# A new order for one unit of an attention kernel: value products two steps at a time, other TensorE work placed between raw score pairs

## The chip, the cores and the metric

The kernel runs on one core of a Trainium2 chip. The metric is the device time of one execution in microseconds, the median of several runs. The engines are TensorE (PE, with its weight loads as PEld), VectorE (DVE), ScalarE (ACT), GpSimd (POOL) and SyncE (SP), which here only issues transfers.

## What is computed

A cross-attention over 8 batches of 256 channels by 512 positions with 16 heads of 16 channels, followed by a mixture of experts (8 experts, two chosen for each of 2048 rows). Cut to what matters here:

```python
q = Wq @ target + bq; k = Wk @ source + bk; v = Wv @ source + bv     # target is layernorm(x)
dot = einsum('bhdt,bhds->bhts', q, k) / sqrt(16)
dot = mask * dot - (1 - mask) * 1e6
out = einsum('bhts,bhds->bhdt', softmax(dot) * mask, v)
x = x + out
x = x + experts(layernorm(x))          # softmax gate, top 2 of 8, silu(g) * u, down projection
```

## The kernel before

**Units.** The attention is cut into 16 units, one for each 128 rows (8 heads) of each batch. Units 0 and 1 have orders of their own (the start); units 2 to 15 run `unit(u)`, once on each engine, and unit 15 is the `TAIL`. Behind the last unit come the experts, whose code the change does not touch but for one product.

**What TensorE does in a unit.** A unit has eight steps s of four heads or blocks j. `scores(u, s, j)` makes one 128x512 tile of transposed scores in one of three banks `sc`; ScalarE takes its exponential into the buffer `pr` of the step; `product(u, s)` multiplies the four tiles of a step with the values, four 32-column products side by side, accumulated in the bank `pvb`. Four steps make one half of the unit's output, which ScalarE copies to `ov`. In the same unit TensorE makes the *raw* scores of a later unit, `raw_scores(u, w, m)`, 16 pairs of 128x512 for each unit, of which VectorE takes the maxima (`maximum`, one reduction for each pair). The maxima go through a transposition (`transpose_maxima`), a split into three bf16 parts on VectorE (`split_maxima`) and a transfer (`keep_maxima` on SP) into rows of `qk`, and `scores(u + 1, 0, 0)` waits for them.

**The pairs.** Unit u makes the pairs m = 4 to 15 of unit u + 1 and then m = 0 to 3 of unit u + 2. I count them i = 0 to 15 within a unit, so that i = 12 is the first pair of unit u + 2. It waits for that unit's rows of `qk`: `pe.wait_ge(stacked[m // 8].sem, ...)` for m = 0, which is the landing of `stack(u + 2, 0)`; i = 4 waits in the same way for `stack(u + 1, 1)`.

**Other TensorE work of a unit.** `values` (16 small f32 products), `project(u, 0)` and `project(u, 1)` (query and key projections of unit u + 3), `transpose_tokens`, `logits` and `ranks` (the expert choice of unit u - 2). They and the raw pairs share two PSUM buffers `tile` in turn: a tile may be written when VectorE (for `transpose_tokens`, ScalarE) has read the tile before the last one.

**What sets the order.** All orders are written out by hand, one for each engine, and an engine's queue runs in order. SP's order in a unit is

```python
store_product(u - 1, 1); keep_split(u, 1); load_product(u); store_x1(u)
store_recip(u)          # waits for rec_made "m", which reciprocals(u, 1) on VectorE raises
stack(u + 2, 0)         # two transfers, of 768 KB and of 8 KB
store_product(u, 0); load_recip(u); keep_split(u, 0); keep_maxima(u + 1, ALL)
```

(left out: its waits, and what comes first, `stack(u + 1, 1)` and loads). `reciprocals(u, 0)` and `reciprocals(u, 1)` are two small VectorE instructions on the softmax denominators of unit u - 1. In the profile `maximum` is L990, the second reciprocal instruction L974, `store_recip` L507, `stack` L453 and L456, `keep_maxima` L526, `scores` L1507, `raw_scores` L1519, `product` L1545.

Of the kernel before, what the change touches and what calls it, by code (L numbers as in the profile page):

```python
# [8 lines left out]
BF16 = mybir.dt.bfloat16  # L9
# [8 lines left out]
P = 128  # L18
# [30 lines left out]
VALUES_AT = 1, 0  # L49
NSLOT = 2  # L50
# [49 lines left out]
def pairs_of(n, s):  # L100

    if 0 <= n < len(FRONT):
        at = 3 * s if s < 4 else 2 * s + 4
        return FRONT[n][at:at + (3 if s < 4 else 2)]
    first = LEAD + 2 * s
    w, m = (n + 1, first) if first < NPAIR else (n + 2, first - NPAIR)
    return [(w, m), (w, m + 1)] if has(w) else []


def maxima_of(n, s):  # L110

    front = {(0, 1): (0, 1), (0, 4): (1, 0), (1, 1): (1, 1)}
    if (n, s) in front:
        return [front[n, s]]
    return [(n + 1, ALL)] if n > 0 and s == 6 and has(n + 1) else []
# [6 lines left out]
def fillers(n, s):  # L122

    return ((["v"] if s == VALUES_AT[n > 0] and has(n + 1) else []) + (["q"] if s == 3 and has(n + 3) else [])
            + (["xT"] if s == 3 and has(n - 2) else []) + (["logits"] if s == 4 and has(n - 2) else []))


def tile_events(n):
    ev = []
    for s in range(8):  # L130
        max_ = [(n, ("max", *pair)) for pair in pairs_of(n, s)]
        ev += max_[:1]
        if s == 7 and has(n - 2):
            ev.append((n, "ranks"))
        ev += max_[1:]
        ev += [(n, name) for name in fillers(n, s)]
# [5 lines left out]
        if s == 7 and has(n + 3):  # L142
            ev.append((n, "k"))
        if n == TAIL and s == 2:
            ev.append((n, "early"))
        if n == LAST - 1 and s == 7:
            ev.append((n, "count"))
# [70 lines left out]
def attention(nc, load_expert, x, ctxt, mask, maskc, maskd, wq, wk, wv, bq, bk, bv, gate, ident, ut, iotas,  # L218
# [3 lines left out]
    with st:  # L222
# [14 lines left out]
        mall = sb("mall", [B, T])  # L237
        mrow = sb("mrow", [B, 2, T], BF16)
# [13 lines left out]
        pr = [sb(f"pr{i}", [P, 4, T]) for i in range(2)]  # L252
        ov = sb("ov", [P, 2, T])
        mx = sb("mx", [P, 2, 32])
# [82 lines left out]
        def of(ahead, *names):  # L337
# [12 lines left out]
                for h in range(2)]  # L350
# [33 lines left out]
                 (mall[:, :], mask, mask_in))  # L384
# [265 lines left out]
        def _(pool):  # L650
# [160 lines left out]
        def _(act):  # L811
# [94 lines left out]
        def _(dve):  # L906
# [250 lines left out]
            def unit(u):  # L1157
                maximum(u, u + 1, 4)
                normalize(u - 1)
                maximum(u, u + 1, 5)  # L1160
                values_out(u)

                maximum(u, u + 1, 6)
                token_stats(u, 0)
                maximum(u, u + 1, 7)
                token_stats(u, 1)

                maximum(u, u + 1, 8)
                token_normalize(u, 0)
                maximum(u, u + 1, 9)  # L1170
# [670 lines left out]
```

## Time and profile before

| what | value |
|---|---|
| median of 3 runs | 869.19 us (865.51 to 871.01) |
| the profiled execution, as timed | 871.53 us |
| its span on the core | 869.7 us |
| TensorE busy | 801.8 us, 92% |
| VectorE busy | 553.6 us, 64% |
| ScalarE busy | 318.6 us, 37% |
| GpSimd busy | 370.3 us, 43% |
| mean granted clock of TensorE | 0.972 |

The profile is one execution; its busy times are shares of the span. What the time is worth in a unit is read from the stretches of that unit, since the start, the attention units and the experts have different limits. The units 2 to 13 take from 121.85 to 504.85 us, the experts from about 557 us to the end.

### The profile page before, as it was taken

How to read it: one execution, taken by the hardware profiler on the slowest of the kernel's cores; microseconds unless marked ns; L12 is line 12 of the kernel's file. 1: busy time of each engine (PE TensorE's matmuls, PEld its weight loads, DVE VectorE, ACT ScalarE, POOL GpSimd, SP SyncE). 2: the span in 40 equal slices, each digit the busy share in tenths (PEclk: the TensorE clock that was granted, in tenths of full speed). 3: DMA queues.
4: the chain of work that ended last, by engine and by line, in shares of the span. 5: the costliest groups of instructions: out<-in, count | busy, mean ns of one | idle time of the engine just before them, and what ended most of it. 6: DMA issues, size and time to landing. Idle time of an engine off the chain costs nothing. (4 is left out here: it accounts for less than half of the span.)

```text
span 869.7 us, 13002 instructions
## 1 busy us (share of the span) xinstructions
PE 801.8 (92%) x3757; PEld 365.1 (42%) x3758; DVE 553.6 (64%) x1071; ACT 318.6 (37%) x619; POOL 370.3 (43%) x392
## 2 busy tenths in 40 slices
PE   5888898989999998999989988899999999999993
PEld 2322332333333433433333332365555665665661
DVE  5778887889888887888877874445433333333331
ACT  0035465556565565665655666522000000000000
POOL 7544364556565655655745423334211221211221
PEclk9579999999999999999999999999999999999997
DMA  6745577666766866856845542354648546354332
GB/s 188 231 129 145 172 203 221 200 209 210 231 206 184 264 196 182 257 163 177 244 127 160 172 113 83 94 144 110 152 89 227 133 110 172 65 156 72 72 51 34
DMA packets 84524, 138.02 MB, mean 159 GB/s; under 512 B 14765, under 2 KB 40685, under 8 KB 84474
## 3 DMA queue, kind: packets, MB, share of 16 engines
q1 hardware_dynamic: 68970, 108.65, 41.8%
q0 software_dynamic: 7744, 17.86, 10.7%
q10 hardware_dynamic: 7760, 10.89, 4.5%
q8 instruction: 25, 0.41, 0.2%
q14 instruction: 25, 0.20, 0.1%
HBM read 77.36 MB, written 59.36 MB: 157 GB/s over the span
## 5 line engine op out<-in xcount | busy, mean ns | idle before, releaser
L843 ACT ACTIVATE pr<-sc 128x512 f32<-128x512 f32 x512 | 267.1, 603 | 219.5 <-PE sc L1507 219.3
L990 DVE TENSOR_REDUCE mx<-tile 128x2 f32<-128x1024 f32 x256 | 309.0, 1216 | 55.9 <-PE tile L1519 50.3
L1507 PE MATMUL sc<-qk 100*128 100x512 bf16 x512 | 154.8, 384 | 9.9 <-DMA qk<-mxt 7.2
L1519 PE MATMUL tile<-qk 97*128 97x512 bf16 x496 | 150.9, 388 | 14.0 <-DVE mx L990 7.9
L765 POOL DMA_INDIRECT out_dram<-xin,ids x36 | 56.4, 1566 | 224.0 <-DVE ids L1312 220.0
L1545 PE MATMUL pvb<-pr,vp 128*32 128x512 f32 x1024 | 138.0, 611 | 0.0
L1660 PE MATMUL pvb<-wring,qkf 128*128 (+1 forms) x216 | 98.7, 593 | 1.6 <-DVE qkf L1322 1.6
L720 POOL TENSOR_SCALAR parts<-qkf 128x512 bf16<-128x512 f32 x31 | 46.9, 1512 | 123.3 <-DVE qkf L1074 119.3
L1519 PEld LDWEIGHTS tile<-qk 97*128 97x128 bf16 x496 | 35.0, 98 | 145.6 <-issue 75.7
L1639 PE MATMUL tile<-wring,xh 128*128 x288 | 91.3, 460 | 0.0
L1639 PE MATMUL sc<-wring,xh 128*128 x288 | 91.2, 459 | 0.0
L1507 PEld LDWEIGHTS sc<-qk 100*128 100x128 bf16 x512 | 49.4, 100 | 91.1 <-ACT pr L843 41.2
L1328 DVE TENSOR_SCALAR xin<-pvb,metay 128x512 f32<-128x512 f32 x36 | 27.0, 750 | 68.4 <-PE pvb L1660 68.4
L1639 PEld LDWEIGHTS sc<-wring,xh 128*128 128x128 f32 x288 | 53.1, 190 | 30.9 <-issue 7.7
L1639 PEld LDWEIGHTS tile<-wring,xh 128*128 128x128 f32 x288 | 53.0, 190 | 30.7 <-issue 7.7
L1660 PEld LDWEIGHTS pvb<-wring,qkf 128*128 128x128 f32 (+1 forms) x216 | 41.0, 190 | 43.7 <-issue 36.3
L877 ACT ACTIVATE xh<-sc 128x352 f32<-128x352 f32 x18 | 8.4, 465 | 127.4 <-PE sc L1639 127.4
L877 ACT ACTIVATE xh<-tile 128x352 f32<-128x352 f32 x18 | 8.4, 465 | 124.3 <-PE tile L1639 124.3
L725 POOL TENSOR_SCALAR parts<-rest 128x512 bf16<-128x512 f32 x31 | 46.4, 1498 | 2.7
L735 POOL TENSOR_TENSOR att<-num,rb 128x512 f32<-128x512 f32 x16 | 20.5, 1282 | 58.5 <-DMA rb<-recip_d 58.5
L1320 DVE COPY qkf<-sc 128x256 f32<-128x256 f32 x36 | 15.3, 424 | 46.9 <-PE sc L1650 42.3
L1561 PE MATMUL tile<-xh,wq_s 128*128 128x512 f32 x64 | 33.3, 645 | 10.0 <-DMA bqk<-bq_dram 7.7
(158 smaller groups left out, 789.1 us busy)
## 6 DMA issues: line engine op xcount, KB each, us to landing
qk<-stack_d SPq DMA_DIRECT2D x32, 768.0 KB
stack_d<-parts SPq DMA_DIRECT2D x32, 384.0 KB, 3.1
wring<-w_dram SPq DMA_DIRECT2D x32, 352.0 KB, 7.2
cin<-routed_d ACTq DMA_DIRECT2D x36, 257.0 KB, 3.6
stack_d<-parts SPq DMA_DIRECT2D x32, 256.0 KB, 3.1
pv_d<-ov SPq DMA_DIRECT2D x32, 256.0 KB, 3.4
xin<-x_dram SPq DMA_DIRECT2D x16, 256.0 KB, 5.4
cin<-ctxt_dram SPq DMA_DIRECT2D x8, 512.0 KB, 6.3
```

Source lines behind the costliest of these rows:

```text
L720: pool.tensor_scalar(parts[:, side, 0, :], src, 1.0, None, ALU.mult).then_inc(done.sem, 1)
L725: pool.tensor_scalar(parts[:, side, 1, :], rest[:, side, :], 1.0, None, ALU.mult).then_inc(done.sem, 1)
L765: pool.indirect_dma_start(out, bass.IndirectOffsetOnAxis(ap=ids[:, k, :], axis=0), y[:, k, :], None, compute_op=ALU.add).then_inc(y_added, 16)
L843: nc.scalar.activation(pr[s % 2][:, j, :], sc[(32 * u + 4 * s + j) % NSC][:, :], ACT.Exp, scale=SCALE).then_inc(exped.sem, 1)
L990: dve.tensor_reduce(cols, t[:, :, :], X, ALU.max, negate=True).then_inc(drained.sem, 1)
L1328: dve.tensor_scalar(y[:, k, :], dp, metay[:, k, 0:1], None, ALU.mult).then_inc(y_made, 1)
L1507: nc.tensor.matmul(sc[(32 * u + 4 * s + j) % NSC][:, :], ks[half(u)][0:ALL_ROWS, h, c * P:c * P + P], qs[half(u)][0:ALL_ROWS, h, :], start ...
L1519: last = nc.tensor.matmul(t[:, i, :], qs[half(w)][0:RAW_ROWS, h, c * P:c * P + P], ks[half(w)][0:RAW_ROWS, h, :], start=True, stop=True)
L1545: last = nc.tensor.matmul(pvb[32 * i:32 * i + 32, :], vp[half(u)][:, c, 4 * g + i, :], pr[s % 2][:, i, :], start=(c == 0), stop=(c == 3))
L1561: last = nc.tensor.matmul(t[:, 0, :], weight[:, c, half(w) * P:half(w) * P + P], source[:, parity(w), c, :], start=(c == 0), stop=(c == 1))
L1639: last = nc.tensor.matmul(dst[:, 0:I], xtl[k][:, c, :], wring[:, bass.ds(off + (c * 2 * I + o), I)], start=(c == 0), stop=(c == 3))
L1660: last = nc.tensor.matmul(dp, acT[0:w, c, :], wring[0:w, bass.ds(off + (W1N + c * T), T)], start=(c == 0), stop=(c == len(ICHUNKS) - 1))
```

## The change

TensorE's unit is written out anew. Raw pairs are spread among the scores, the projection of queries stands between the pairs 6 and 7, the value products come in blocks of two steps (6 and 7 of the unit before, 0 and 1, 2 and 3, 4 and 5), and `ranks` and the key projection stand behind the last step's first scores. Since a product now comes up to three steps behind its scores, `pr` has three buffers (`NPR`) in place of two; to make room, the mask's start-up tiles lie in `ov`. VectorE's unit is reordered to match, with `reciprocals(u, 1)` behind the pair 10, `split_maxima` ahead of most of `choose`, and `projection_out(u, 1)` ahead of the pairs 14 and 15. On GpSimd `token_rstd` goes ahead of `values_out`. SP's order and ScalarE's order stay as they are. Units 0 and 1 keep their order under the name `front`. Cut to its core:

```diff
+NPR = 3
+STEADY = (0, 1, 2, "v", 3, 4, 5, 6, "q", 7, "xT", 8, 9, 10, "logits", 11, 12, 13, "maxT", "k", "ranks", 14, 15)
...
+def pair_of(n, i):
+    m = LEAD + i
+    return (n + 1, m) if m < NPAIR else (n + 2, m - NPAIR)
...
+        mall = ov[0:B, 0, :]
+        mrow = ov[0:B, 1, :].bitcast(BF16).rearrange("b (s t) -> b s t", s=2)
...
             for u in range(1, UNITS):
                 if has(u + 2):
                     part(u, 1)
+                if has(u - 2):
+                    token_rstd(u)
                 if has(u + 1):
                     values_out(u)
-                if has(u - 2):
-                    token_rstd(u)
                 if has(u - 3):
...
-                            if j == 0 and (due := pved.at(u, s, back=2)) is not None:
+                            if j == 0 and (due := pved.at(u, s, back=NPR)) is not None:
                                 act.wait_ge(pved.sem, due)
-                            nc.scalar.activation(pr[s % 2][:, j, :], sc[(32 * u + 4 * s + j) % NSC][:, :],
+                            nc.scalar.activation(pr[(8 * u + s) % NPR][:, j, :], sc[(32 * u + 4 * s + j) % NSC][:, :],
...
             def unit(u):
-                maximum(u, u + 1, 4)
+                maximum(u, *pair_of(u, 0))
                 normalize(u - 1)
-                maximum(u, u + 1, 5)
+                maximum(u, *pair_of(u, 1))
+                maximum(u, *pair_of(u, 2))
+                token_stats(u, 0)
+                token_stats(u, 1)
                 values_out(u)
-                maximum(u, u + 1, 6)
-                token_stats(u, 0)
-                maximum(u, u + 1, 7)
-                token_stats(u, 1)
-                maximum(u, u + 1, 8)
+                maximum(u, *pair_of(u, 3))
                 token_normalize(u, 0)
-                maximum(u, u + 1, 9)
+                maximum(u, *pair_of(u, 4))
+                maximum(u, *pair_of(u, 5))
                 token_normalize(u, 1)
                 if u == TAIL:
                     plan_early()
-                maximum(u, u + 1, 10)
+                maximum(u, *pair_of(u, 6))
                 reciprocals(u, 0)
-                maximum(u, u + 1, 11)
+                projection_out(u, 0)
+                maximum(u, *pair_of(u, 7))
+                maximum(u, *pair_of(u, 8))
+                batch_stats(u, 0)
+                maximum(u, *pair_of(u, 9))
+                batch_stats(u, 1)
+                maximum(u, *pair_of(u, 10))
                 reciprocals(u, 1)
-                projection_out(u, 0)
-                maximum(u, u + 1, 12)
-                maximum(u, u + 1, 13)
                 choose(u, 0)
                 choose(u, 1)
+                maximum(u, *pair_of(u, 11))
+                maximum(u, *pair_of(u, 12))
+                maximum(u, *pair_of(u, 13))
                 choose(u, 2)
+                split_maxima(u, u + 1, ALL)
                 choose(u, 3)
-                maximum(u, u + 1, 14)
-                batch_stats(u, 0)
-                maximum(u, u + 1, 15)
-                batch_stats(u, 1)
                 choose(u, 4)
                 choose(u, 5)
                 if u == TAIL:
                     fetch(0, 0)
-                maximum(u, u + 2, 0)
-                maximum(u, u + 2, 1)
-                split_maxima(u, u + 1, ALL)
-                maximum(u, u + 2, 2)
+                projection_out(u, 1)
                 rows_of(u, 0)
-                maximum(u, u + 2, 3)
                 rows_of(u, 1)
-                projection_out(u, 1)
+                maximum(u, *pair_of(u, 14))
+                maximum(u, *pair_of(u, 15))
...
+            def raw(u, i):
+                w, m = pair_of(u, i)
+                if has(w):
+                    raw_scores(u, w, m)
...
+            def unit(u):
+                scores(u, 0, 0)
+                scores(u, 0, 1)
+                scores(u, 0, 2)
+                raw(u, 0)
+                scores(u, 0, 3)
+                if u > len(FRONT):
+                    product(u - 1, 6)
+                product(u - 1, 7)
+                raw(u, 1)
+                scores(u, 1, 0)
+                raw(u, 2)
+                scores(u, 1, 1)
+                scores(u, 1, 2)
+                scores(u, 1, 3)
+                values(u)
+                scores(u, 2, 0)
+                raw(u, 3)
+                scores(u, 2, 1)
+                scores(u, 2, 2)
+                raw(u, 4)
+                scores(u, 2, 3)
+                scores(u, 3, 0)
+                raw(u, 5)
+                scores(u, 3, 1)
+                product(u, 0)
+                product(u, 1)
+                raw(u, 6)
+                project(u, 0)
+                scores(u, 3, 2)
+                raw(u, 7)
+                scores(u, 3, 3)
+                scores(u, 4, 0)
+                scores(u, 4, 1)
+                if u == TAIL:
+                    count_early()
+                transpose_tokens(u)
+                scores(u, 4, 2)
+                raw(u, 8)
+                scores(u, 4, 3)
+                raw(u, 9)
+                product(u, 2)
+                product(u, 3)
+                scores(u, 5, 0)
+                raw(u, 10)
+                scores(u, 5, 1)
+                scores(u, 5, 2)
+                logits(u)
+                scores(u, 5, 3)
+                raw(u, 11)
+                if u == TAIL:
+                    transpose_rows(0, 0)
+                scores(u, 6, 0)
+                raw(u, 12)
+                scores(u, 6, 1)
+                scores(u, 6, 2)
+                scores(u, 6, 3)
+                raw(u, 13)
+                product(u, 4)
+                product(u, 5)
+                if has(u + 1):
+                    transpose_maxima(u, u + 1, ALL)
+                scores(u, 7, 0)
+                project(u, 1)
+                scores(u, 7, 1)
+                scores(u, 7, 2)
+                scores(u, 7, 3)
+                ranks(u)
+                raw(u, 14)
+                raw(u, 15)
...
-            for u in range(UNITS):
+            for u in range(len(FRONT)):
+                front(u)
+            for u in range(len(FRONT), UNITS):
                 unit(u)
...
             off = gate(0, 0)
+            product(TAIL, 6)
             product(TAIL, 7)
```

TensorE in a unit of even number, step 6 up to the transposed maxima. Before (`pvb` is written by a product, `tile` by a raw pair, L1626 is the transposition of the maxima):

```order
L1507 MATMUL sc1<-qk0 128x512
L1507 MATMUL sc2<-qk0 128x512
L1507 MATMUL sc0<-qk0 128x512
L1519 MATMUL tile0<-qk0 128x512 x2
L1507 MATMUL sc1<-qk0 128x512
L1545 MATMUL pvb<-pr1,vp0 32x512 x4
L1519 MATMUL tile1<-qk0 128x512 x2
L1626 MATMUL tile0<-idf,mx 32x128
L1507 MATMUL sc2<-qk0 128x512
```

The same place in the changed kernel (scores are L1520, raw pairs L1532, products L1558, the transposed maxima L1639):

```order
L1520 MATMUL sc1<-qk0 128x512
L1532 MATMUL tile0<-qk0 128x512 x2
L1520 MATMUL sc2<-qk0 128x512
L1520 MATMUL sc0<-qk0 128x512
L1520 MATMUL sc1<-qk0 128x512
L1532 MATMUL tile1<-qk0 128x512 x2
L1558 MATMUL pvb<-pr2,vp0 32x512 x4
L1558 MATMUL pvb<-pr0,vp0 32x512 x4
L1639 MATMUL tile0<-idf,mx 32x128
L1520 MATMUL sc2<-qk0 128x512
L1574 MATMUL tile1<-cin,wk_s 128x512 x2
```

The product of one step between the two raw pairs is gone, a block of two stands behind the second pair, and the key projection follows the transposed maxima.

VectorE around the reciprocals (L968 and L974 before; the tile reductions are L990). Before:

```order
L990 TENSOR_REDUCE mx<-tile0 128x2
L968 RECIPROCAL rec<-den 128x32
L990 TENSOR_REDUCE mx<-tile1 128x2
L974 TENSOR_TENSOR rec<-rec,md 128x32
L1074 SCALAR_TENSOR_TENSOR qkf<-tile0,bqk,mb 128x512
L990 TENSOR_REDUCE mx<-tile0 128x2
```

In the changed kernel (reciprocals L981 and L987, reductions L1003):

```order
L981 RECIPROCAL rec<-den 128x32
L1087 SCALAR_TENSOR_TENSOR qkf<-tile0,bqk,mb 128x512
L1003 TENSOR_REDUCE mx<-tile1 128x2 x2
L931 BN_STATS ln<-xin 128x6
L1003 TENSOR_REDUCE mx<-tile0 128x2
L934 BN_AGGR ln<-ln 128x2
L1003 TENSOR_REDUCE mx<-tile1 128x2
L987 TENSOR_TENSOR rec<-rec,md 128x32
```

The second reciprocal instruction stood one reduction behind the first (behind the pair 7); now four reductions, the drain of the query projection and the statistics of an input stand between them (behind the pair 10).

## Rows read from the trace of the kernel before

**Rows 1.** The page, part 1: busy time, share of the span and instructions of each engine.

```profile
PE 801.8 (92%) x3757; PEld 365.1 (42%) x3758; DVE 553.6 (64%) x1071; ACT 318.6 (37%) x619; POOL 370.3 (43%) x392
```

**Rows 2.** Timeline, TensorE: the first scores of units 2, 6 and 14.

```profile
start us, us, engine line op out<-in xcount [idle before <-releaser]
121.85 0.82 PE L1507 MATMUL sc<-qk 100*128 100x512 bf16 x3
...
252.27 0.81 PE L1507 MATMUL sc<-qk 100*128 100x512 bf16 x3
...
504.85 0.82 PE L1507 MATMUL sc<-qk 100*128 100x512 bf16 x3 [1.40 <-DMA qk<-mxt]
```

**Rows 3.** Timeline of unit 6: TensorE's kinds of work, and one reduction.

```profile
255.10 1.95 PE L1572 MATMUL tile<-wv_s,cin 128*128 128x128 f32 x16
256.89 0.81 PE L1507 MATMUL sc<-qk 100*128 100x512 bf16 x3
...
265.62 1.98 PE L1561 MATMUL tile<-xh,wq_s 128*128 128x512 f32 x4
...
267.44 0.60 PE L1584 MATMUL tile<-idf,xa 128*128 128x128 f32 x4
...
268.53 0.60 PE L1519 MATMUL tile<-qk 97*128 97x512 bf16 x2
...
268.97 0.38 PE L1507 MATMUL sc<-qk 100*128 100x512 bf16 x1
...
269.27 1.07 PE L1545 MATMUL pvb<-pr,vp 128*32 128x512 f32 x8
...
270.27 0.60 PE L1519 MATMUL tile<-qk 97*128 97x512 bf16 x2
...
270.92 1.23 DVE L990 TENSOR_REDUCE mx<-tile 128x2 f32<-128x1024 f32 x1 [0.53 <-PE tile L1519]
```

**Rows 4.** Timeline, from the reciprocal to the stack and its reader, units 6 and 13.

```profile
265.75 1.16 DVE L990 TENSOR_REDUCE mx<-tile 128x2 f32<-128x1024 f32 x1
...
266.83 0.17 DVE L974 TENSOR_TENSOR rec<-rec,md 128x32 f32<-128x32 f32 x1
267.03 0.32 SPq L507 DMA_DIRECT2D recip_d<-rec  x1
...
267.46 0.38 SPq L453 DMA_DIRECT2D qk<-stack_d  x1
...
489.86 0.38 SPq L453 DMA_DIRECT2D qk<-stack_d  x1
...
496.98 0.61 PE L1519 MATMUL tile<-qk 97*128 97x512 bf16 x2 [0.94 <-DMA qk<-mrow_d]
```

**Rows 5.** SP's own waits: us in total, times, longest us.

```profile
SPq L507 <- DVE rec L974: 28.0, 9, 5.8
```

**Rows 6.** Timeline, transposed maxima, their split and the next scores, units 8, 13, 14.

```profile
341.11 0.27 DVE L1003 CAST mxt<-tile 32x128 bf16<-32x128 f32 x1
...
347.46 0.82 PE L1507 MATMUL sc<-qk 100*128 100x512 bf16 x3 [1.69 <-DMA qk<-mxt]
...
500.52 0.27 DVE L1003 CAST mxt<-tile 32x128 bf16<-32x128 f32 x1
...
527.81 0.28 PE L1626 MATMUL tile<-idf,mx 128*32 128x128 f32 x1
...
528.13 0.28 DVE L1003 CAST mxt<-tile 32x128 bf16<-32x128 f32 x1 [1.00 <-PE tile L1626]
```

**Rows 7.** Timeline and windows (PE busy, PEclk, DMA share, GB/s) of a stall in unit 2.

```profile
131.90 0.64 PE L1519 MATMUL tile<-qk 97*128 97x512 bf16 x2 [1.77 <-DMA qk<-mrow_d]
132.34 0.62 PE L1507 MATMUL sc<-qk 100*128 100x512 bf16 x1
...
135.59 0.90 PE L1507 MATMUL sc<-qk 100*128 100x512 bf16 x3
...
132.00:134.00 2.00, 2.00 (x11) 0.58 1.03 387
134.00:136.00 2.00, 2.00 (x8) 0.56 0.82 287
```

More of the change, by code:

```diff
@@ L100, in pairs_of, with front_events @@
 def pairs_of(n, s):
[L102 to L107, printed above, removed]
+    at = 3 * s if s < 4 else 2 * s + 4
+    return FRONT[n][at:at + (3 if s < 4 else 2)]
+def pair_of(n, i):
+    m = LEAD + i
+    return (n + 1, m) if m < NPAIR else (n + 2, m - NPAIR)
 def maxima_of(n, s):
[L112 to L115, printed above, removed]
+    front = {(0, 1): (0, 1), (0, 4): (1, 0), (1, 1): (1, 1), (1, 6): (2, ALL)}
+    return [front[n, s]] if (n, s) in front else []
 def heads_of(g):
     return slice(0, UH) if g == ALL else slice(4 * g, 4 * g + 4)
[L122 to L128, printed above, removed]
+def front_events(n):
     ev = []
@@ L131, in tile_events @@
         max_ = [(n, ("max", *pair)) for pair in pairs_of(n, s)]
[L132 to L136, printed above, removed]
+        ev += max_
+        if s == VALUES_AT[n]:
+            ev.append((n, "v"))
+        if s == 3:
+            ev.append((n, "q"))
         if n == 0 and s == 0:
@@ L141, in tile_events @@
         ev += [(n, ("maxT", *part)) for part in maxima_of(n, s)]
-        if s == 7 and has(n + 3):
+        if s == 7:
             ev.append((n, "k"))
-        if n == TAIL and s == 2:
-            ev.append((n, "early"))
-        if n == LAST - 1 and s == 7:
-            ev.append((n, "count"))
+    return ev
+def tile_events(n):
+    if 0 <= n < len(FRONT):
+        return front_events(n)
+    ahead = {"v": 1, "q": 3, "k": 3, "xT": -2, "logits": -2, "ranks": -2, "maxT": 1}
+    ev = []
+    for name in STEADY:
+        if name == "xT" and n == TAIL:
+            ev.append((n, "early"))
+        if name == "maxT":
+            if has(n + 1):
+                ev.append((n, ("maxT", n + 1, ALL)))
+        elif name in ahead:
+            if has(n + ahead[name]):
+                ev.append((n, name))
+        elif has(pair_of(n, name)[0]):
+            ev.append((n, ("max", *pair_of(n, name))))
+    if n == LAST - 1:
+        ev.append((n, "count"))
     return ev
@@ L251, in attention @@
         vp = [sb(f"vp{i}", [P, 4, UH, 32]) for i in range(2)]
-        pr = [sb(f"pr{i}", [P, 4, T]) for i in range(2)]
+        pr = [sb(f"pr{i}", [P, 4, T]) for i in range(NPR)]
         ov = sb("ov", [P, 2, T])
+        mall = ov[0:B, 0, :]
+        mrow = ov[0:B, 1, :].bitcast(BF16).rearrange("b (s t) -> b s t", s=2)
         mx = sb("mx", [P, 2, 32])
@@ L1545, in product @@
                     last = nc.tensor.matmul(pvb[32 * i:32 * i + 32, :], vp[half(u)][:, c, 4 * g + i, :],
-                                            pr[s % 2][:, i, :], start=(c == 0), stop=(c == 3))
+                                            pr[(8 * u + s) % NPR][:, i, :], start=(c == 0), stop=(c == 3))
                 last.then_inc(pved.sem, 1)
@@ L1662, in down, with front @@
                 last.then_inc(down_done, 1)
-            def unit(u):
+            def raw(u, i):
+                w, m = pair_of(u, i)
+                if has(w):
+                    raw_scores(u, w, m)
+            def front(u):
                 for s in range(8):
                     todo = pairs_of(u, s)
-                    if has(u):
-                        scores(u, s, 0)
-                        scores(u, s, 1)
-                    if has(u):
-                        scores(u, s, 2)
+                    scores(u, s, 0)
+                    scores(u, s, 1)
+                    scores(u, s, 2)
                     for w, m in todo[:1]:
                         raw_scores(u, w, m)
-                    if has(u):
-                        scores(u, s, 3)
-                    if s == 0 and has(u - 1):
+                    scores(u, s, 3)
+                    if s == 0 and u:
                         product(u - 1, 7)
-                    if s and has(u):
+                    if s:
                         product(u, s - 1)
-                    if s == 7:
-                        ranks(u)
                     for w, m in todo[1:]:
                         raw_scores(u, w, m)
-                    if s == VALUES_AT[u > 0]:
+                    if s == VALUES_AT[u]:
                         values(u)
@@ L1691, in unit @@
                         project(u, 0)
-                        transpose_tokens(u)
-                    if u == TAIL and s == 2:
-                        count_early()
-                    if s == 4:
-                        logits(u)
-                    if u == TAIL and s == 5:
-                        transpose_rows(0, 0)
                     for w, g in maxima_of(u, s):
```

4 lines of the change are left out of this document (1 added, 3 removed).

## The prediction

> **What bounds the kernel now.** I read the page first: TensorE is busy 92% of the span and no other engine is above 64% [rows 1], so time is made or lost on TensorE, either in work it need not do or in stretches where it waits. Then the timeline by units [rows 2]: units 2 to 13 take 504.85 - 121.85 = 383.0 us, 31.9 us each, so a microsecond in a unit is worth 12 in the total. Then what TensorE's instructions cost when nothing waits [rows 3], and last who holds the transfers on which TensorE depends [rows 4 to 6]. The reader is to see in rows 4 that the stack of unit u + 2 is already only just in time.
>
> **Prices on TensorE [rows 3].** Starts tell more than durations, since a matmul overlaps the next. A raw pair takes 268.97 - 268.53 = 0.44 us and a score half of that, 0.22. The values take 256.89 - 255.10 = 1.79, the query projection 267.44 - 265.62 = 1.82 (0.1 of it a wait inside, so 1.72), the token transposes 0.44. One product step, from its last score to the next raw pair, takes 270.27 - 268.97 = 1.30; less the score's own 0.22 that is 1.08. It holds two f32 passes for four column groups side by side. A pass of a 512-column f32 matmul pair in the projection is 1.72 / 4 = 0.43, so 0.86 of 1.08 is streaming and about 0.22 is entering and leaving the mode of narrow columns.
>
> **What blocks of two save.** If the second product follows without a gap, a block takes 2 x 0.86 + 0.22 = 1.94 us instead of 2.16, a saving of 0.22. Units 3 to 15 have four such blocks, unit 2 three, and one stands behind unit 15: 56 x 0.22 = 12.3 us. The bounds are 0 (the second product pays its own entry) and 0.30 (the raw pair behind a block starts sooner). I take 0.22. The same count, scores, pairs and blocks added up, must reproduce the kernel before: ahead of the pair i = 7 there stand 16 scores, 7 pairs, 4 single blocks and the values, 3.5 + 3.1 + 4.3 + 1.8 = 12.7 us. The trace has unit 6 start at 252.27 [rows 2] and that pair's reduction at 265.75 [rows 4], which is 13.5, and a reduction starts 0.65 behind its pair (270.92 - 270.27) [rows 3]. 12.7 + 0.65 = 13.4: the count holds.
>
> **What moves: the second reciprocal.** This is the term that decides. In SP's order `store_recip(u)` stands ahead of `stack(u + 2, 0)`, and it waits for VectorE's second reciprocal instruction. In unit 6 that starts at 266.83, 14.56 us into the unit; SP issues the recip at 267.03 and the stack at 267.46, 0.63 behind the instruction's start [rows 4]. SP is shown waiting for that instruction 9 times, 28.0 us in all [rows 5]. The stack's rows are needed by the pair i = 12. In unit 13 that pair starts 496.98 - 489.86 = 7.1 us behind the issue and was held by the landing for 0.94 us [rows 4]. So there is no slack in it.
>
> The changed VectorE order puts this instruction behind the pair 10 instead of the pair 7. Ahead of the pair 10 TensorE now has 21 scores (4.6), 10 pairs (4.4), three blocks of two (5.8), values, projection and transposes (1.79 + 1.72 + 0.44): 18.8 us. With reductions of 1.08 (266.83 - 265.75) to 1.14 [rows 3, 4] laid beside it, TensorE also waits for a tile ahead of the values and of pairs 5 and 8, 0.6 us together by my layout. So the pair 10 starts at 19.4, its reduction at 20.0, the reciprocal at 21.1 and the stack's issue at 21.1 + 0.63 = **21.8** us into the unit, instead of 15.2.
>
> Without a wait the pair 12 would follow pair 10 by two pairs, four scores and the logits, about 2.7 us, at 22. It now waits for a landing. How long the stack takes is bounded above by unit 13's 7.1 us, exactly the landing there, and below by that pair's unwaited start in other units, which shows only that it can be less; I put the lower end at 5.5 and take 6.5, nearer the row. So the pair 12 starts at **28.3**, after a stall of about 6 us. Queued behind it on TensorE are three scores, the pair 13, the block 4 and 5 and the transposed maxima; ScalarE runs dry for want of scores, and VectorE for want of tiles. Nothing else fills the stall, since TensorE's queue is in order.
>
> **From the pair 12 to the next unit.** Pair, three scores, pair, block: 0.44 + 0.65 + 0.44 + 1.94 = 3.5 us to the transposed maxima, at 31.8. From there a second chain decides: the split starts 528.13 - 527.81 = 0.32 behind the transposition, and the next unit's first score comes 504.85 - 500.52 = 4.33 behind the split's start in unit 13, 347.46 - 341.11 = 6.35 in unit 8 [rows 2, 6], both held by the transfer. TensorE's own work there (four scores, the key projection, ranks, two pairs) is 4.0 us, so it now waits about 0.7 of 4.65 us; before, the same work was 5.7 and hid most of the chain. I take 4.65, since after a stall few other transfers are under way, and keep 6.35 as the bound.
>
> **The clock.** In unit 2 TensorE was idle for 1.77 us [rows 7]. The granted clock then fell to half, the lower of its two levels (1.2 instead of 2.4 GHz), in the two stretches shown (0.58 and 0.56). From the score at 132.34 to that at 135.59 are 3.25 us for work (score, block, pair) that takes 1.30 + 0.44 = 1.74 at full clock [rows 3, 7]: 1.5 us lost. A stall of 6 us is longer than that one, so I expect the fall in every such unit, and take 1.5 us for it; the bounds are 0 (it rises again before the work) and 3.5 (all 3.5 us behind the pair 12 run at half).
> By the Trainium skill, TensorE: Matmul & The Clock Gate, Part 1, the throttled state is the default and activity releases it. By that rule alone a stall this long would be followed by slow work until it is released; the trace agrees in unit 2, and the rule is the ground of the third rival.
>
> **The sum.** A unit takes 21.8 + 6.5 + 3.5 + 1.5 + 4.65 = 38.0 us. Units 2 to 13 all stack rows for a unit u + 2: 12 x 38.0 = 456. Unit 2 keeps its old stall and its fall of the clock, 1.8 + 1.5 = 3.3, which come ahead of the new one. Unit 13 has no query projection, so 1.7 less. That is 457.6 instead of 383.0, **+74.6 us**, with the blocks' saving inside it. Units 14 and 15 and the last product have no stack to wait for: their blocks save about 2 us, and the early count of routed rows, issued in step 4 instead of 2, may give as much back. I enter 0. The start and the experts are unchanged at 0, hidden or not, since no instruction of theirs moves. The new buffers for the exponentials cost nothing: the waits they relax are on ScalarE, busy 37% [rows 1]. GpSimd's swap of two steps is worth nothing while it is idle over half the span. The profiled execution was timed at 871.5, so it becomes 946; it lies 2.3 above the median of the runs, which gives **943 us**.
>
> **The rivals.**
> First, *shorter stalls*: the stack lands in 5.5 us, with little else under way, and the clock costs nothing. Then a unit takes 38.0 - 1.0 - 1.5 = 35.5, and the time is 943 - 12 x 2.5 = 913. For it: TensorE's stall leaves the memory to the stack alone. Against: rows 4 and 7.
> Second, *the stack is not on the path*, and the blocks' saving is what remains: 869 - 12 = 857, faster. Its mechanism is that SP reaches `store_recip` late for another reason, so that moving the reciprocal costs nothing. It decides in its favour only if the stack's issue stays before about 15.5 us into the unit. For it: SP's wait is shown in 9 of 16 cases, not in all. Against: SP cannot issue the stack ahead of an instruction that is itself 6.5 us later in the order; the queue is in order and the wait is still there. Only an error in my count of VectorE's order could make it true.
> Third, *a longer fall of the clock*: the work from the pair 12 to the transposed maxima runs at half throughout, 3.5 us instead of 1.5. The time is 943 + 12 x 2.0 = 967. For it: the stall is over three times as long as the one in rows 7.
> Fourth, *the second chain*: if the maxima's transfer takes unit 8's time in every unit, 12 x 2.0 = 24 more, again 967. Against: after the stall the queue is empty.
>
> **Chances and range.** My forecast (930 to 955) 0.55, shorter stalls 0.15, a longer fall or the longer chain 0.22, no stall at all 0.04, the rest for something smaller on either side that I have not seen. The range reaches from the first rival to the third, 913 to 968. About 1% is what a measurement of this kernel can tell from no change: faster by more 0.04, within 1% 0.02, slower by more 0.94.
>
> **What the profile after would show.** The second reciprocal starts 21 us into a unit, not 14.6, and the stack is issued 0.6 behind it. The first raw pair of step 6 has an idle time of 5 to 7 us before it, released by the transfer into `qk`. PEclk shows dips throughout the attention part; TensorE's share falls below 88%. The first scores of a unit wait for the transfer of the maxima in nearly all units. Blocks of 16 product matmuls take 1.9 us. I am wrong if the stack is issued before 18 us, if the pair 12 starts without a wait, or if units take under 34 us.

## The result and the profile after

The changed kernel takes 954.87 us in the median (953.59 to 955.22, 4 runs), the kernel before beside it 868.12 us (865.51 to 871.01, 4 runs): a ratio of 1.0996, with a 95% interval of 1.0957 to 1.1035. It is 10% slower. The prediction said 943 us, between 913 and 968, and slower. The profiled execution took 953.59 us, with a span of 951.8 and a mean granted clock of 0.925.

The page after, busy time by engine and the slices of TensorE and of its clock, answers to [rows 1]:

```profile
PE 824.6 (87%) x3757; PEld 379.4 (40%) x3758; DVE 550.6 (58%) x1071; ACT 326.1 (34%) x619; POOL 370.8 (39%) x392
...
PE   5889897797987977979879778879999999999993
...
PEclk9589997998988988989889889989999999999997
```

The instructions of each engine are as many as before. VectorE and GpSimd are busy as long as before, to within 3 us, ScalarE 7.5 us longer; that is no effect of the stalls, since e7, without them, shows 326.3 as well. TensorE is busy 22.8 us longer by the records of slowed matmuls, and its share has fallen, so there is new idle time and a lower clock, both in the attention part: the last third of the slices is untouched.

Who waited for what, of the kernel after, in us, times and longest; SP's row answers to [rows 5]:

```profile
PE tile L1532 <- DMA qk<-mrow_d: 66.8, 13, 6.3
SPq L520 <- DVE rec L987: 146.2, 16, 12.8
POOL att L748 <- DMA rb<-recip_d: 144.7, 16, 20.1
```

The wait of 28.0 us in 9 cases of SP for the second reciprocal has become 146.2 in 16, and behind it TensorE waits 66.8 us in 13 cases for the load that ends the stack. One such stall, in unit 7, which starts at 313.02 (timeline of the kernel after: start, duration, engine and line), answers to [rows 4]:

```profile
334.19 0.18 DVE L987 TENSOR_TENSOR rec<-rec,md 128x32 f32<-128x32 f32 x1
334.39 0.32 SPq L520 DMA_DIRECT2D recip_d<-rec  x1
334.83 0.36 SPq L466 DMA_DIRECT2D qk<-stack_d  x1
335.23 0.59 SPq L469 DMA_DIRECT2D qk<-mrow_d  x1
340.28 1.03 PE L1532 MATMUL tile<-qk 97*128 97x512 bf16 x2 [5.13 <-DMA qk<-mrow_d]
341.11 1.49 PE L1520 MATMUL sc<-qk 100*128 100x512 bf16 x3
342.39 1.06 PE L1532 MATMUL tile<-qk 97*128 97x512 bf16 x2
343.38 2.38 PE L1558 MATMUL pvb<-pr,vp 128*32 128x512 f32 x16
345.69 0.28 PE L1639 MATMUL tile<-idf,mx 128*32 128x128 f32 x1
346.01 0.28 DVE L1016 CAST mxt<-tile 32x128 bf16<-32x128 f32 x1 [1.16 <-PE tile L1639]
...
350.35 0.82 PE L1520 MATMUL sc<-qk 100*128 100x512 bf16 x3 [0.55 <-DMA qk<-mxt]
```

Read it from the top: the stack is issued 334.83 - 313.02 = 21.81 us into the unit and the pair i = 12 starts 5.45 behind that. The pair and the three scores then take 1.03 and 1.49 us where undisturbed ones take 0.60 and 0.81 as records [rows 3]: that is the lower clock level, a granted clock of 0.50 from 338 to 344. The last row is the next unit's first score, 350.35 - 345.69 = 4.66 behind the transposed maxima. Units 2 to 13 run from 122.13 to 578.47, **456.3 us** instead of 383.0; units 3 to 12 take 37.3 to 39.7 each, and in all ten the stack is issued 21.80 or 21.81 us into the unit.

### The profile page after: what moved, and what is told of

It reads as the page before. It is cut to its first block and busy times, and to the rows that moved or that the text cites. A ratio compares the mean times of both kernels' runs of the same rounds, so it can differ in the third digit from the quotient of the medians.

```text
span 951.8 us, 13001 instructions
## 1 busy us (share of the span) xinstructions
PE 824.6 (87%) x3757; PEld 379.4 (40%) x3758; DVE 550.6 (58%) x1071; ACT 326.1 (34%) x619; POOL 370.8 (39%) x392
## 5 line engine op out<-in xcount | busy, mean ns | idle before, releaser
L1003 DVE TENSOR_REDUCE mx<-tile 128x2 f32<-128x1024 f32 x256 | 306.0, 1219 | 121.9 <-PE tile L1532 115.8
L856 ACT ACTIVATE pr<-sc 128x512 f32<-128x512 f32 x512 | 274.4, 602 | 262.9 <-PE sc L1520 236.6
L1532 PE MATMUL tile<-qk 97*128 97x512 bf16 x496 | 158.9, 410 | 74.8 <-DMA qk<-mrow_d 66.8
L1520 PE MATMUL sc<-qk 100*128 100x512 bf16 x512 | 170.6, 404 | 11.7 <-DMA qk<-mxt 9.1
L1558 PE MATMUL pvb<-pr,vp 128*32 128x512 f32 x1024 | 136.4, 648 | 0.0
L1532 PEld LDWEIGHTS tile<-qk 97*128 97x128 bf16 x496 | 39.6, 101 | 168.8 <-DMA qk<-mrow_d 73.3
L1520 PEld LDWEIGHTS sc<-qk 100*128 100x128 bf16 x512 | 51.9, 104 | 111.7 <-issue 36.7
L1652 PE MATMUL sc<-wring,xh 128*128 x288 | 91.2, 459 | 0.0
L748 POOL TENSOR_TENSOR att<-num,rb 128x512 f32<-128x512 f32 x16 | 20.2, 1264 | 144.7 <-DMA rb<-recip_d 144.7
L1558 PEld LDWEIGHTS pvb<-pr,vp 128*32 128x32 f32 x1024 | 27.6, 117 | 72.7 <-issue 54.3
```

Source lines behind the costliest of these rows:

```text
L748: pool.tensor_tensor(att[:, :], num[:, :], rb[:, :], ALU.mult).then_inc(post.sem, 1)
L856: nc.scalar.activation(pr[(8 * u + s) % NPR][:, j, :], sc[(32 * u + 4 * s + j) % NSC][:, :], ACT.Exp, scale=SCALE).then_inc(exped.sem, 1)
L1003: dve.tensor_reduce(cols, t[:, :, :], X, ALU.max, negate=True).then_inc(drained.sem, 1)
L1520: nc.tensor.matmul(sc[(32 * u + 4 * s + j) % NSC][:, :], ks[half(u)][0:ALL_ROWS, h, c * P:c * P + P], qs[half(u)][0:ALL_ROWS, h, :], start ...
L1532: last = nc.tensor.matmul(t[:, i, :], qs[half(w)][0:RAW_ROWS, h, c * P:c * P + P], ks[half(w)][0:RAW_ROWS, h, :], start=True, stop=True)
L1558: last = nc.tensor.matmul(pvb[32 * i:32 * i + 32, :], vp[half(u)][:, c, 4 * g + i, :], pr[(8 * u + s) % NPR][:, i, :], start=(c == 0), sto ...
```

## The experiments

**Is it the place of the second reciprocal? e1 takes that back in the kernel after, e2 does it alone in the kernel before.**

```diff
# e1_rec_back, on the kernel after
                 maximum(u, *pair_of(u, 7))
+                reciprocals(u, 1)
                 ...
                 maximum(u, *pair_of(u, 10))
-                reciprocals(u, 1)
# e2_rec_late_in_before, on the kernel before
                 maximum(u, u + 1, 11)
-                reciprocals(u, 1)
                 ...
                 maximum(u, u + 1, 14)
+                reciprocals(u, 1)
```

> The changed kernel with one VectorE instruction back in its old place: the second reciprocal stands behind the pair 7, not the pair 10. My theory (SP holds the stack behind the reciprocal's store, and the pair 12 waits for the stack): the reciprocal runs about 16 us into a unit, the stack is issued at 16.7 instead of 21.8, lands at 22.7, and the pair 12 waits under 1 us instead of 5 to 6, without a fall of the clock behind it. A unit takes about 31 us instead of 38, the time is 865 to 880. Rival (TensorE's own new order or VectorE's load is what costs, the stack only shows it): the stall stays or turns up at another pair, and the time stays above 930.

> The kernel before with only the second reciprocal moved behind the pair 10, TensorE's order untouched. My theory: the reciprocal at about 21.7 us into a unit, the stack issued at 22.3, landed at 28.3; the pair 12 stood at 22.8, so it waits 5 to 6 us, and the clock falls; some of the old wait ahead of the transposed maxima goes. A unit takes 37.5 to 39.5 us instead of 31.9, the time is 935 to 960. Rival (the new TensorE order is needed for the loss): under 885.

Measured: e1 885.44 us, 1.0162 [1.0103, 1.0221] of before; e2 951.01, 1.0938 [1.0907, 1.0968]. So one line of VectorE's order moves the kernel before by 82 us and gives back 69 of the changed kernel's 87. The rival in which the place of the reciprocal costs nothing is dead. In e2 SP waits 151.0 us in 16 cases for it, as in the kernel after. By the traces 77.8 of e2's 80.0 us are in units 2 to 13 (460.8 us); its unit 15 also takes 4.5 us more than before up to its last score, so the late reciprocal reaches the tail too. e1 stays 17 us above before and 5 above its expected range, where the blocks' saving should have put it below. The timeline of e1, of unit 6 from 252.49 on, shows part of why:

```profile
268.47 0.18 DVE L987 TENSOR_TENSOR rec<-rec,md 128x32 f32<-128x32 f32 x1
268.68 0.32 SPq L520 DMA_DIRECT2D recip_d<-rec  x1
269.11 0.42 SPq L466 DMA_DIRECT2D qk<-stack_d  x1
269.58 0.59 SPq L469 DMA_DIRECT2D qk<-mrow_d  x1
...
274.92 0.61 PE L1532 MATMUL tile<-qk 97*128 97x512 bf16 x2 [0.30 <-DMA qk<-mrow_d]
...
283.30 0.82 PE L1520 MATMUL sc<-qk 100*128 100x512 bf16 x3 [0.81 <-DMA qk<-mxt]
```

The stack is still only just in time, and the next unit's first score still waits for the maxima. Units 2 to 13 take 385.4 us, 2.4 more than before. Unit 15 takes 31.27 us up to its last score where before it took 22.42: most of the rest of e1's loss is in that tail, to which e7 comes back.

**Is it the stack, or the reciprocals' own readers? e3 leaves VectorE's order as changed and lets SP pass the stack first.** `stack(u + 2, 0)` with its two waits moves ahead of `store_recip(u)`, which waits for the reciprocal, for u > 1 (its old place keeps it for u < 2 alone, left out here):

```diff
+                if u > 1 and has(u + 2):
+                    sp.wait_ge(split_kept[0].sem, split_kept[0].at(u - 1, "k"))
+                    sp.wait_ge(split_kept[1].sem, split_kept[1].at(u, "k"))
+                    stack(u + 2, 0)
                 if has(u - 1):
                     store_recip(u)
```

> The changed kernel with the reciprocal left late, but on SP the stack of unit u + 2 goes ahead of the reciprocal's store (units 2 to 13). My theory: the late reciprocal itself harms nobody on TensorE, only its place in SP's queue does. The stack is then held by the scores of step 3 (it overwrites rows that they read), so it is issued about 15.2 us into a unit and lands at 21 to 22; the pair 12 waits for at most 0.5 us. A unit takes 30 to 31 us, the time is 855 to 872. Rival (the late reciprocal delays the residual and what hangs on it by as much): above 900, with VectorE waiting for GpSimd at the token statistics.

Measured: 876.88 us, 1.0110 [1.0077, 1.0144]. 78 of the 87 us are back with the reciprocal as late as ever, so the damage goes through SP's queue: the transfer that stood behind the wait, not the late value itself. It is 5 us above the expected range, and by its trace that is not in the steady units: units 2 to 13 take 378.3 us, 4.7 less than before, but unit 15 takes 29.71 up to its last score and unit 14 takes 30.67 instead of 28.47, so here too the tail of e7 weighs most. Its timeline shows a smaller cost that neither theory had. The late reciprocal puts the residual's two operations on GpSimd beside short instructions of VectorE. In units 2 to 12 these are mostly instructions of `choose`, behind the split of the maxima, and TensorE's rank matmuls wait there for its result `selb` 6.6 us in 8 cases; in unit 13 it is the split itself (line numbers are 4 higher than in the kernel after):

```profile
491.82 1.26 POOL L752 TENSOR_TENSOR att<-num,rb 128x512 f32<-128x512 f32 x1 [11.52 <-DMA rb<-recip_d]
491.94 1.22 DVE L1024 CAST mxt<-mxr 32x128 bf16<-32x128 f32 x1
493.16 1.26 POOL L760 TENSOR_TENSOR x<-att,xr 128x512 f32<-128x512 f32 x1
493.20 1.37 DVE L1026 TENSOR_TENSOR mxt<-mxr,mxt 32x128 bf16<-32x128 f32 x1
```

The same cast takes 0.215 us and the same subtraction 0.280 in the median of the 7 instances in the stretch 300 to 500, this one included. Here each ends 0.08 and 0.15 us behind the end of GpSimd's operation, and TensorE's rank matmul behind them waits 2.53 us for VectorE. By the Trainium skill, SBUF — State Buffer, Who interferes with whom, VectorE and GpSimd share a pair of ports as an exclusive lock, which a VectorE instruction needs when it runs in a two-port mode, which a cast can, or has two SBUF inputs while GpSimd reads SBUF; the rows fit, since the cast reads and writes SBUF and the subtraction has two inputs there, though no row shows the cast's mode. VectorE's reductions, whose one input is in PSUM, keep their time beside the same two operations: in e7 three of them take 3.49 us from 327.80 on, with GpSimd's residual running from 328.28 to 330.91.

**What does the lower clock cost? e4 fills the stall.** 24 extra raw matmuls, whose results the pair i = 12 overwrites, stand ahead of the stack's wait in units 2 to 13; nothing is left out.

```diff
+                for i in range(fill):
+                    nc.tensor.matmul(t[:, i % 2, :], qs[half(w - 1)][0:RAW_ROWS, 7, 3 * P:4 * P],
+                                     ks[half(w - 1)][0:RAW_ROWS, 7, :], start=True, stop=True)
+                if fill:
+                    pe.wait_ge(stacked[0].sem, stacked[0].at(w - 2, "g"))
```

(left out: `fill` is 24 for the pair m = 0 where u > 1, else 0, and the old wait stands only where it is 0.)

> The changed kernel with 24 extra raw matmuls into the tile of the pair 12 ahead of its wait for the stack, in units 2 to 13; the real pair overwrites them. They fill about 5.2 us of the stall. My theory (the fall of the clock behind the stall costs 2 to 3 us in a unit beside the stall itself): the granted clock stays at 1.0 and the work from the pair 12 to the transposed maxima takes 3.5 us instead of 5 to 6.6; the time falls by 20 to 36 us, to 919 to 935. Rival (the half clock is hidden by the next chain or by ScalarE): no change, 950 to 958.

Measured: 932.32 us, 1.0726 [1.0694, 1.0757]. Unit 7, which starts at 304.59 there, has the fill, the pair i = 12 and its scores at

```profile
326.56 5.34 PE L1533 MATMUL tile<-qk 97*128 97x512 bf16 x24
...
332.11 0.60 PE L1539 MATMUL tile<-qk 97*128 97x512 bf16 x2 [0.21 <-DMA qk<-mrow_d]
...
332.55 0.81 PE L1521 MATMUL sc<-qk 100*128 100x512 bf16 x3
```

The stack is issued 21.81 us into this unit too and the pair follows 5.7 behind it (5.9 in the mean of units 3 to 12, 5.8 in the kernel after), so the stall is as long as in the kernel after, only filled, and the granted clock stays at its upper level from 54.12 on for 498 us. Units 2 to 13 take 431.1 us instead of 456.3: the clock costs **2.1 us a unit** there, 25.2 of the 73.3 that these units lose, and the rest is waiting. The whole kernel gains only 22.6, since in e4 the units 14 and 15 take 4.9 us more together, with falls of the clock of their own. By the Trainium skill, TensorE: Matmul & The Clock Gate, Part 1, the throttled state is the default and activity releases it; this run agrees, since work without any use kept the level up.

**What holds the rest? e5, e6 and e7 take the remaining causes away one upon the other.**

```diff
# e5_rec_next, on the kernel after (VectorE)
                 reciprocals(u, 0)
+                reciprocals(u, 1)
                 ...
-                reciprocals(u, 1)
# e6_recip_load, on e5 (SP)
-                if has(u):
-                    store_product(u, 0)
                 if has(u - 1):
                     load_recip(u)
+                if has(u):
+                    store_product(u, 0)
# e7_count_early, on e6 (TensorE): from step 4 back to the end of step 2
                 scores(u, 2, 3)
+                if u == TAIL:
+                    count_early()
                 ...
-                if u == TAIL:
-                    count_early()
```

> The changed kernel with the second reciprocal directly behind the first (behind the pair 6). My theory: SP is then held by the scores of step 3 alone and issues the stack about 15.2 us into a unit; the pair 12 waits at most 0.5 us. The residual on GpSimd starts when the loaded reciprocals land, and its two instructions may meet the split of the maxima on VectorE, which then takes 1 us more. A unit takes 30.5 to 31.5 us, the time is 868 to 880. Rival (the late reciprocal explains only part of the loss, as the first experiment ended at 885): not below 882.

> As the run before, and on SP the load of the reciprocals goes ahead of the store of the unit's first product. My theory (VectorE's short copies are held for 1.2 us while GpSimd runs one of the residual's two instructions): these now run about 3 us earlier and end before the split of the maxima; copies of 1.2 us in the split disappear, and a unit takes 0.5 to 1 us less, the time falls by 6 to 12 us against the run before. Rival (those long copies wait for something else, or are hidden by the transfer of the maxima): less than 2 us.

> As the run before, and in the last unit the early count of routed rows is issued at the end of step 2, as it was before the change, instead of in step 4. My theory (the tail's loss is the wait for the first expert rows, whose addresses hang on that count): the wait of 4.7 to 4.8 us ahead of the first row transposes shrinks to under 1.5 us and the fall of the clock behind it goes; the time falls by 4 to 7 us. Rival (that wait is set by the routing of the rows or by SP's queue): less than 1.5 us.

Measured: e5 881.19, 1.0145 [1.0109, 1.0182], 1 us outside its expected range; e6 868.91, 1.0010 [0.9983, 1.0037]; e7 862.59, 0.9942 [0.9916, 0.9967]. The median of e5 is 4.3 us under that of e1, but the runs overlap (877.0 to 885.7 and 877.6 to 887.5) and so do the intervals of their ratios: that the reciprocal right behind the first gives more than e1's place is not shown. Letting SP load the reciprocals ahead of the product's store, which waits for ScalarE, gives 12.3: GpSimd's wait for them falls from 91.2 to 65.1 us, each in 15 cases, the residual comes before the split, and units 2 to 13 fall from 379.1 to 368.4 us, the worst two, 6 and 7, from 32.7 and 33.8 to 30.3 and 30.6. What the split gains is in the traces. Unit 4 of e5:

```profile
210.25 1.26 POOL L756 TENSOR_TENSOR x<-att,xr 128x512 f32<-128x512 f32 x1
...
210.44 1.15 DVE L1020 CAST mxt<-mxr 32x128 bf16<-32x128 f32 x1
```

In 11 of the units 2 to 13 of e5 that cast ends 0.08 us behind GpSimd's operation, and in the twelfth the subtraction behind it ends 0.14 behind. In units 3 to 13 the cast takes 0.21 to 1.15 us in e5, 0.66 in the median, and 0.21 to 0.24 in e6. In all the split gets 6.4 us shorter in units 2 to 13, of the 10.7 that these units gain.

The early count gives 6.3. These are the rows of unit 15 that it moves, of the kernel after and then of e7 (in e7 the unit starts at 518.89, after at 607.07):

```profile
619.25 0.17 PE L1627 MATMUL tile<-before,ones 128*128 128x8 bf16 x1
...
629.19 1.11 PE L1647 MATMUL tile<-idf,cin 128*128 128x128 f32 x4 [4.71 <-DMA cin<-routed_d]
```

```profile
527.33 0.21 PE L1627 MATMUL tile<-before,ones 128*128 128x8 bf16 x1
...
537.39 0.66 PE L1647 MATMUL tile<-idf,cin 128*128 128x128 f32 x4
```

The count runs 12.2 us into the unit instead of 8.4. That delayed the plan and so the load of the first expert's rows, issued 19.5 us into the unit instead of 15.8, and TensorE, whose order has the row transposes next, stood idle for them. In e7 unit 15 takes 23.3 us up to its last score; it took 29.05 after and 22.42 before.

**What is a block of two worth? e8 splits each of the four blocks of e7 by a score.**

```diff
                 product(u, 4)
+                scores(u, 7, 0)
                 product(u, 5)
                 if has(u + 1):
                     transpose_maxima(u, u + 1, ALL)
-
-                scores(u, 7, 0)
```

and the same at the other three places.

> As the run before, with one score between the two products of each block in units 2 to 15, so that each product enters and leaves the narrow columns by itself; no work is added. My theory: 0.22 us more for each of 56 blocks, 12 us if TensorE sets the pace everywhere; where a unit waits for the transfer of the maxima anyway some of it is hidden, so 6 to 12 us more. Rival (a block of two saves nothing): no difference.

Measured: 878.25, 1.0120 [1.0092, 1.0148], 15.7 us more than e7, or 0.28 for each of the 56 blocks, above the 6 to 12 us expected. A split block of e8:

```profile
326.62 1.07 PE L1558 MATMUL pvb<-pr,vp 128*32 128x512 f32 x8
327.62 0.39 PE L1520 MATMUL sc<-qk 100*128 100x512 bf16 x1
327.94 1.06 PE L1558 MATMUL pvb<-pr,vp 128*32 128x512 f32 x8
328.93 0.61 PE L1532 MATMUL tile<-qk 97*128 97x512 bf16 x2
```

From 326.62 to 328.93 are 2.31 us, less 0.22 for the score 2.09. A block of 16 in the kernel after, from 616.09 to the next score at 617.94, takes 1.85: 0.24 less. All 40 blocks in units 3 to 12 of e8 and of e7 agree with these to 0.01 us. So the prediction's 0.22 was about right for the block itself, and 56 x 0.24 = 13.4 of the 15.7 us are that. By the Trainium skill, TensorEngine Tiling (Array Packing), Key Properties, changing the tiling mode drains TensorE; it gives no price, and 0.24 is what splitting a block costs here. By the two profiled executions the difference in units 2 to 13 is larger, 385.9 us against 366.4, where the 47 blocks account for 11.3; e8's weight loads for scores also wait longer for ScalarE (31.8 us against 13.2 from 184 to 458), so the split costs something beside the entry, and how much of that reaches the time is open. And e8, the new order with its three repairs but without blocks, is 1.2% slower than the kernel before: no run here shows a gain from spreading the raw pairs.

**Does the chain from the maxima to the next unit set the unit's length? e9 shortens it in e7.**

```diff
                 product(u, 4)
-                product(u, 5)
                 if has(u + 1):
                     transpose_maxima(u, u + 1, ALL)
+                product(u, 5)
```

> The run that counts early (the best so far), with the transposition of the maxima between the two products of the block 4 and 5. My theory: the transposition comes 0.8 us earlier, but VectorE has the reductions 11 to 13 in a row and starts the split only 0.3 us earlier; the split block costs 0.2 to 0.3. In units 2 to 12 the two cancel; in units 13 and 14, where VectorE is free, the next unit starts up to 0.8 us earlier. The time falls by 0 to 4 us. Rival (the chain from the transposition sets the unit's length everywhere): 0.7 us in each of 14 units, 9 us less.

Measured: 853.45 us, **0.9814** [0.9787, 0.9841]. It is the fastest version of all, 1.9% faster than the kernel before. Its median is 9.1 us under e7's, where 0 to 4 was my expectation; the kernel before ran 1.8 us slower beside e9 than beside e7, and measured against it the gain is 11.0. By its time the rival, that the chain sets the length of every unit, has won; its trace says otherwise. Of e7, then of e9, the waits of TensorE in the steady units (183 to 458), and the end of unit 13:

```profile
PE sc L1520 <- DMA qk<-mxt: 6.6, 10, 1.3
...
487.19 1.46 PE L1520 MATMUL sc<-qk 100*128 100x512 bf16 x3 [1.37 <-DMA qk<-mxt]
488.44 1.06 PE L1532 MATMUL tile<-qk 97*128 97x512 bf16 x2
```

```profile
PE sc L1520 <- DMA qk<-mxt: 1.6, 5, 0.8
...
487.62 0.82 PE L1520 MATMUL sc<-qk 100*128 100x512 bf16 x3 [1.14 <-DMA qk<-mxt]
488.27 0.60 PE L1532 MATMUL tile<-qk 97*128 97x512 bf16 x2
```

The wait for the maxima went from 6.6 to 1.6 us, but units 3 to 12 take 304.6 us instead of 305.4. The loads of the raw pairs' weights wait more for VectorE's reductions (24.1 us in 59 cases against 20.2 in 52), and VectorE is busy for 239.0 of 273.3 us there: what the chain no longer takes, waits for the reductions seem mostly to take. The two spans differ by 4.8 us, 853.0 against 857.8, and most of that, 3.7, is in unit 14: in e7 the clock falls behind the 1.37 us wait (the second row at 1.06 us), in e9 it does not (0.60). The runs differ the same way: e7's 12 have mean granted clocks of 0.962 to 0.974 and its fastest, 858.91, had 0.974; e9's 6 have 0.970 to 0.977. Shorter waits seem to be worth mainly the falls of the clock that they avoid. But the length of the wait alone does not decide it: in the kernel before, the waits of 1.40 us ahead of unit 14 [rows 2] and of 1.69 [rows 6] were followed by no fall (granted clock 1.00 from 503 to 511 and from 346 to 352), while e7's 1.37 was. The account is read from two traces and the clocks of 18 runs and was not tried by itself: how many of the 9.1 us it explains stays open.

**Do the two repairs help the kernel before? e10** puts its second reciprocal directly behind the first and its `load_recip` ahead of `store_product`:

```diff
                 reciprocals(u, 0)
-                maximum(u, u + 1, 11)
                 reciprocals(u, 1)
+                maximum(u, u + 1, 11)
```

> The kernel before with the second reciprocal directly behind the first and, on SP, the load of the reciprocals ahead of the store of the unit's first product; TensorE's order untouched. My theory: the stack is issued 1 us earlier (14.2 us into a unit), the waits for it in units 7 and 13 go; the residual on GpSimd runs from about 22 to 24.4 us into a unit and still meets the choice's short instructions, so the wait ahead of the transposed maxima stays in part. The time falls by 1 to 5 us. Rival (these two repairs, and not the new TensorE order, make the whole gain of the best version): the time falls by 5 us or more, to 863 or less.

Measured: 868.02 us, 0.9972 [0.9944, 1.0001]. In the new order the load alone is worth 12.3 us; in the old the two together are worth 1.7, not to be told from nothing. So e9's gain comes from the new order with its faults removed, above all from the blocks of two, not from the repairs alone.

## Why the prediction was right, and which term was mis-sized

*The step that decides.* The second reciprocal behind the pair 10, SP's wait, the stack behind that wait: shown by e1, e2 and e3. The counted layout gave the stack's issue at 21.8 us into a unit; the trace has 21.80 or 21.81 in all of units 3 to 12.

*The stall.* Landing was put at 6.5; units 3 to 13 show 5.4 to 6.6, in unit 7 5.45, and 5.8 in the mean of units 3 to 12. The pair i = 12 was to wait about 6 us; TensorE was idle 5.0 to 6.3 us ahead of it.

*The clock.* Put at 1.5, measured by e4 at 2.1. In the trace the lower level, granted from within the stall on, holds for 6.83 us in ten of the twelve units and for 10.24 in units 2 and 8. From the pair 12 to the transposed maxima the units 3 to 12 take 5.7 us in the mean where the prediction had 3.5 + 1.5 = 5.0. Landing too long by 0.7 and clock too short by 0.7 cancel, which is why a unit came out at 37.3 to 39.7 us, 38.0 in the mean, and units 2 to 13 at 456.3 for 457.6. That agreement is partly luck. Unit 2's old stall was to cost 3.3; it shrank to a wait of 0.98 us with no fall of the clock behind it, and the unit took 39.7 instead of 41.3.

*From transposition to next unit.* 4.65 forecast, 4.66 in unit 7. The third rival (all work behind the pair at half) is seen in unit 8 and nearly in unit 2, where the maxima follow 6.65 and 6.23 us behind the pair; the fourth (the longer chain in each unit) is not seen. Of the first, the shorter landing came true in unit 7, but its free clock is refuted by e4, and the second rival by e1 and e2.

*The blocks.* 0.22 forecast, 0.24 in the rows of e8 and the kernel after, 0.28 by their times. It was never visible in the total, since the unit's length came from the stack.

*The tail: the mis-sized term.* I entered 0 for units 14 and 15, with the early count taking back what the blocks save. Up to its last score unit 15 went from 22.42 to 29.05 us, +6.6, and e7 gives 6.3 back by moving the count alone: the prediction's sentence that it "may give as much back" as about 2 us named the right instruction and priced it by its own length, not by the plan, the load and TensorE's wait behind it. With 6.6 there and 1.3 less in units 2 to 13, the profiled 946 becomes 951; it was 953.59, and 1.7 of the rest lie behind the attention (315.7 us instead of 314.0), where the prediction entered 0. Its last step is rounded down as well: 946.1 less 2.3 is 943.8, not 943.

*Not seen.* That GpSimd's residual, which follows the reciprocals, collides with VectorE's split (e5 in nearly every unit, e3 in one), and that `load_recip` behind ScalarE's store decides when. The stack's stall hides this in the kernel after, and it appears as soon as the stack is repaired. My expectations for e1, e3 and e5 were 1 to 5 us too low. The tail is the larger part of that: up to its last score unit 15 takes 31.27, 29.71 and 31.79 us there and 22.42 before.

## What to carry to other kernels

In an in-order queue a wait holds every transfer behind it: when an instruction on a compute engine is moved, look up which queue waits for it and what stands behind that wait, and price that, since here moving a 0.18 us instruction cost 82 us. A change that is right in itself (blocks of two, 15.7 us) can be buried by such a side effect, so undo the parts one at a time before the whole is thrown away: three moved lines and one shortened chain turned +10% into -1.9%. Price a moved producer by the chain of its last consumer, above all near the end of a stage where nothing is left to hide it.

## What the hardware showed unexpectedly

Two short VectorE instructions that read and write SBUF took 1.22 and 1.37 us instead of 0.215 and 0.280 beside GpSimd operations of 1.26 us. Their records are longer, not later, so this looks like slow work; that they end 0.08 and 0.15 us behind GpSimd's operations, and the cast 0.08 behind in 11 units of e5, says that it is a wait.

An idle TensorE is not only idle: behind each stall of 5 to 6 us it ran at the lower level of its clock, and that cost 2.1 us a unit. A wait of 1.37 us was followed by a fall in e7's unit 14, one of 1.14 us in e9's was not, and neither were waits of 1.40 and 1.69 in the kernel before: the length of the wait alone does not tell.
